# Experts after a recurrent layer: three of four token groups are normalised and turned behind the recurrent part's last tile, and the first expert's products are halved

## The reference, cut to what matters

```python
h = h + _L1_attn_ref(_layernorm(h), ...)      # the recurrence, all 32 x 192 rows
# step: Qh = h_prev - 2 v (v.h_prev)/(v.v);  h = lam*Qh + (1-lam)*x
h = h + _L1_ffn_ref(_layernorm(h), ...)       # the experts, rows 0..511 only
# gate_up = x[token] @ W_up[expert] + b; inter = (up+1) * gate*sigmoid(1.702*gate)
# down = inter @ W_down[expert] + b; out[token] += weight * down
```

## Time and profile before

| | |
|---|---|
| median of 3 runs | 1030.51 us (1027.21 to 1032.54) |
| the profiled execution | 1034.37 us, span in the trace 1032.6 us |
| PE busy, share of the span | 934.5 us, 91% |
| PE weight loads | 837.2 us, 81% |
| DVE | 786.5 us, 76% |
| ACT | 592.1 us, 57% |
| POOL | 545.4 us, 53% |
| granted clock of PE, mean | 0.957 of full speed |
| DMA | 96.32 MB, 93 GB/s over the span |

### The profile page before, as it was taken

One profiled execution on the slowest core, in us unless ns is written; L12 is line 12 of the kernel. 1 busy time (PEld: TensorE's weight loads), 2 busy tenths in 40 slices (PEclk: granted clock), 3 DMA queues, 4 the chain that ended last, 5 costly groups with the idle time before them and its releaser, 6 DMA issues. The chain is left out here.

```text
span 1032.6 us, 19334 instructions
## 1 busy us (share of the span) xinstructions
PE 934.5 (91%) x5800; PEld 837.2 (81%) x5800; DVE 786.5 (76%) x2393; ACT 592.1 (57%) x1174; POOL 545.4 (53%) x652
## 2 busy tenths in 40 slices
PE   2689999999999999869799999999999999963998
PEld 2689999999999999765587888887888888852887
DVE  3678777777777777652588898988999999972676
ACT  1346666666666666634566676666666666621442
POOL 4156676767676765445244454545555554422573
PEclk9889999999999999988989999999999999975999
DMA  5001111111111140012999999999999999982310
GB/s 208 21 26 42 42 42 41 41 41 41 41 41 41 44 171 22 17 27 76 102 128 142 149 159 139 157 141 152 151 156 150 146 163 141 135 96 94 123 62 21
DMA packets 134814, 96.32 MB, mean 93 GB/s; under 512 B 11208, under 2 KB 129104, under 8 KB 134096
## 3 DMA queue, kind: packets, MB, share of 16 engines
q1 hardware_dynamic: 133200, 91.20, 58.3%
q0 software_dynamic: 1536, 4.20, 1.4%
HBM read 31.92 MB, written 13.11 MB: 44 GB/s over the span
## 5 line engine op out<-in xcount | busy, mean ns | idle before, releaser
L315 POOL TENSOR_TENSOR gelu_lo<-gelu_out,gelu_hi 128x384 fp32r<-128x384 f32 x128 | 151.0, 1208 | 29.9 <-DVE gelu_hi L529 29.4
L944 POOL TENSOR_TENSOR B_decayed_u<-B_scan_in 128x512 f32<-128x512 f32 x48 | 62.0, 1292 | 97.1 <-DMA B_scan_in<-B_stage 88.5
L708 PE MATMUL psA<-ternary_down,gelu_hi 128*128 128x256 f32 x384 | 96.9, 291 | 6.9 <-POOL gelu_lo L315 6.3
L652 PE MATMUL psA<-x2T_hi,ternary_up 128*128 128x384 f32 x256 | 94.7, 370 | 3.4 <-DVE residual L642 3.2
L708 PE MATMUL psA<-ternary_down,gelu_lo 128*128 128x256 f32 x384 | 93.3, 282 | 0.0
L652 PE MATMUL psA<-x2T_lo,ternary_up 128*128 128x384 f32 x256 | 88.5, 346 | 0.0
L932 POOL TENSOR_TENSOR B_y<-B_scan_in,B_states 128x512 f32<-128x512 f32 x48 | 61.9, 1289 | 41.9 <-ACT B_states L1003 41.9
L1192 PEld LDWEIGHTS psB<-B_partial_dots,B_minus_same_batch 128*128 128x128 f32 x384 | 66.4, 194 | 21.8 <-DVE B_partial_dots L1076 10.6
L1180 PE MATMUL psB<-Win_hi,B_x_hi 128*128 128x512 f32 x192 | 83.6, 435 | 0.0
L708 PEld LDWEIGHTS psA<-ternary_down,gelu_hi 128*128 128x128 f32 x384 | 72.2, 188 | 11.4 <-POOL gelu_lo L315 10.2
L1092 DVE SCALAR_TENSOR_TENSOR psB<-B_decayed_u,psB 128x128 f32<-128x128 f32 x192 | 68.0, 354 | 12.7 <-PE psB L1192 12.2
(11 more groups left out here) (251 smaller groups left out, 3329.5 us busy)
## 6 DMA issues: line engine op xcount, KB each, us to landing
B_scan_in<-B_stage SPq DMA_DIRECT2D x192, 256.0 KB, 8.1
patches<-in_patches SPq DMA_DIRECT2D x16, 384.0 KB
B_residual<-layer_out SPq DMA_DIRECT2D x48, 128.0 KB, 5.2
out_dram<-B_residual SPq DMA_DIRECT2D x48, 128.0 KB, 5.0
C_raw<-in_experts SPq DMA_DIRECT2D x8, 768.0 KB, 4.4
layer_out<-residual SPq DMA_DIRECT2D x32, 128.0 KB, 1.8
layer_out<-residual SPq DMA_DIRECT2D x32, 64.0 KB, 2.0
raw_Wl<-in_upT SPq DMA_DIRECT2D x1, 1024.0 KB, 9.1
```

The source lines that it names most:

```text
L315: nc.gpsimd.tensor_tensor(act_l[:, k, :], act[:, k % DEEP, :], act_h[:, k, :].bitcast(F32), ALU.subtract).then_inc(s["ffn_lo"], 1)
L652: last = nc.tensor.matmul(out, a, b, start=(n == 0), stop=(n == len(terms) - 1))
L708: last = nc.tensor.matmul(ps[:, 6 + k // 2, (k % 2) * D:(k % 2 + 1) * D], x[:, c, k * P:(k + 1) * P], dn_w[:, c, :], start=(c == 0 and x i ...
L944: nc.gpsimd.tensor_tensor(lu[:, j % 2], ring[:, j % R_RING, :, LAM, :], ring[:, j % R_RING, :, U, :], ALU.mult).then_inc(s["lu"], 1)
```

## The change

Rows 0..511 are regrouped. Group q = 0, 1, 2 is now steps 0..127 of sequence q, and group 3 is steps 128..191 of sequences 0 and 1. The first three groups are complete once tile 31 is stored, long before part B ends. They become tiles 48, 49 and 50 of part B's normalisation: `has_x` lets the statistics, `rstd`, the normalised rows, the transposes and the split run on for three more tiles, and `x_tiles` puts their halves into part C's operand, which takes the place of the l weights (`Wl_Win_hi`, `Wl_Win_lo`, last used for tile 47). Part C's residual lies in `raw_Wv`, its two raw slots in `raw_Win` and `raw_Wl`, which part B no longer needs by then.

SP issues in part B, at `i = 30`, the constants (14 DMAs where there were 4, since the new groups are pieces of the old ones) and the weights of experts 0 and 1; at `i` = 39, 40 and 41 the rows of the three groups; at `i = 49` the 60 first rows of each half of group 3; and right behind the last residual update two copies of four rows each. ACT makes expert 0's high half at `i = 36`, POOL its low half at `i = 38`. The wait for the last stores moves from part B's end into part C. The semaphores are cleared at part B's start, and the clearing block and its barrier go away.

In part C, expert 0's `gate_up` is made in two halves of 256 columns: the first for groups 0 and 1 at once, then the turn of the routing weights, then the turn of group 3, then the second half. ACT normalises group 3 where DVE did before. The last store is five DMAs, three of them before the last group is done.

```diff
-        l_h, l_l = sb("Wl_Win_hi", [P, DC, DI], F32R), sb("Wl_Win_lo", [P, DC, DI], F32R)
+        l_h, l_l = E.x_h, E.x_l
...
+        def has_x(j):
+            return 0 <= j < TT + 3
+
+        def row_tile(j):
+            return res[:, j % R_RES, :] if j < TT else E.acc[:, j - TT, :]
+
+        def x_tiles(j):
+            if j < TT:
+                return x_h[:, j % 2], x_l[:, j % 2]
+            q = j - TT
+            return E.x_h[:, :, q * P:(q + 1) * P], E.x_l[:, :, q * P:(q + 1) * P]
...
+                if i == TT - 18:
+                    for a, b in ((E.b_up, io["up_bias"]), (E.b_dn, io["down_bias"])):
+                        sp.dma_start(a[:], b).then_inc(E.s["const_in"], 16)
...
+                    for a, b in ((E.picked, io["picked"]), (E.weights, io["routing"])):
+                        for q, lo, hi, q_in, lo_in in ((0, 0, P, 0, 0), (2, 0, P, 3, 0), (1, 0, 64, 1, 64), (1, 64, P, 2, 0),
+                                                       (3, 0, 64, 1, 0), (3, 64, P, 2, 64)):
+                            sp.dma_start(a[lo:hi, q, :], b[lo_in:lo_in + hi - lo, q_in, :]).then_inc(E.s["const_in"], 16)
+                    sp.wait_ge(s["w_lo"], 3)
+                    sp.wait_ge(s["m_ps"], 4)
+                    for e in range(2):
+                        sp.dma_start(E.raw[e], io["experts"][e]).then_inc(E.s["raw_in%d" % e], 16)
+                if i + 9 in range(TT, TT + 3):
...
+                    q = i + 9 - TT
+                    for j in range(28, 32):
+                        wait_stored(sp, j)
+                    sp.dma_start(E.acc[:, q, :], io["out"][q, 0:P, :]).then_inc(res_in[(TT + q) % 8], 16)
+                if i == TT + 1:
...
+                    for j in range(TT - 5, TT - 1):
+                        wait_stored(sp, j)
+                    for b in range(2):
+                        sp.dma_start(E.acc[b * (P // 2):b * (P // 2) + 60, 3, :],
+                                     io["out"][b, P:T - 4, :]).then_inc(E.s["h_in"], 16)
...
+                    if j == TT - 1:
+                        for b in range(2):
+                            sp.dma_start(E.acc[b * (P // 2) + 60:(b + 1) * (P // 2), 3, :],
+                                         res[4 * b:4 * b + 4, j % R_RES, :]).then_inc(E.s["h_in"], 16)
...
+                if i == TT - 10:
+                    pool.wait_ge(E.s["w_hi"], 1)
+                    nc.gpsimd.tensor_tensor(E.w_l[:], E.raw[0], E.w_h[:].bitcast(F32), ALU.subtract).then_inc(E.s["w_lo"], 1)
...
+                if i == TT - 12:
+                    sc.wait_ge(E.s["raw_in0"], 16)
+                    nc.scalar.activation(E.w_h[:], E.raw[0], ACT.Copy).then_inc(E.s["w_hi"], 1)
+                if has_x(i + 4):
...
-                    wait(pe, s["x_lo"], min(i + 5, TT))
+                    wait(pe, s["x_lo"], min(i + 5, TT + 3))
...
-        with nc.Block() as clearing:
-            @clearing.sync
-            def _(sp):
-                for sem_ in s.values():
-                    sp.sem_clear(sem_)
...
+            gate_up(0, slice(0, MT // 2))
+            pe.wait_ge(s["wc"], 1)
+            for q in range(MQ):
+                last = nc.tensor.transpose(ps[0:E_N, 6, q * P:(q + 1) * P], wc[:, q, :], ident[:])
+            last.then_inc(s["wcT"], 1)
+            pe.wait_ge(s["normed"], 1)
+            for c in range(DC):
+                last = nc.tensor.transpose(ps[:, c, 0:P], xn[:, c * P:(c + 1) * P], ident[:])
+            last.then_inc(s["xT"], 1)
+            pe.wait_ge(s["x_lo"], 1)
             for e in range(E_N):
-                gate_up(e)
+                gate_up(e, slice(MT // 2, MT) if e == 0 else slice(0, MT))
```

More of the change, by code:

```diff
@@ L854, in part_b @@
         arrived = [ctx.enter_context(nc.semaphore("B_arrived%d" % q)) for q in range(4)]
[L855 removed]
+        stored = E.stored = [E.stack.enter_context(nc.semaphore("B_stored%d" % q)) for q in range(4)]
+        for name in E.names:
+            E.s[name] = E.stack.enter_context(nc.semaphore("C_" + name))
         def wait_res_in(eng, j):
@@ L1028, in _ @@
                                          ACT.Copy).then_inc(s["y_hi"], 1)
-                if has(i + 4):
+                if has_x(i + 4):
                     j = i + 4
-                    wait(sc, s["z"], j - 1)
+                    wait(sc, s["z"], min(j - 1, TT))
                     sc.wait_ge(s["xT"], j + 1)
-                    nc.scalar.activation(x_h[:, j % 2], XT, ACT.Copy).then_inc(s["x_hi"], 1)
+                    nc.scalar.activation(x_tiles(j)[0], XT, ACT.Copy).then_inc(s["x_hi"], 1)
                 if i == -4:
@@ L1263, in part_c @@
         ident, halfpow = consts.ident, consts.halfpow
[L1264 to L1269, removed]
+        acc, raw, x_h, x_l = E.acc, E.raw, E.x_h, E.x_l
+        picked, weights, b_up, b_dn = E.picked, E.weights, E.b_up, E.b_dn
+        xn = sb("C_normed", [P, D])
+        stats, moments = sb("C_stats", [P, 6]), sb("C_moments", [P, 2])
+        ve, nmean = sb("C_var_eps", [P, 1]), sb("C_minus_mean", [P, 1])
+        rstd, shift = sb("C_rstd", [P, 1]), sb("C_shift", [P, 1])
+        picked_f = sb("C_picked_f", [P, MQ, 2])
         eq = sb("C_is_picked", [P, 2, MQ, E_N])
@@ L1297, in _ @@
         def _(sp):
-            sp.dma_start(acc[:], rows).then_inc(s["h_in"], 16)
-            for a, b in ((picked, io["picked"]), (weights, io["routing"]), (b_up, io["up_bias"]), (b_dn, io["down_bias"])):
-                sp.dma_start(a[:], b).then_inc(s["const_in"], 16)
-            for e in range(E_N):
-                if e >= 2:
-                    sp.wait_ge(s["w_lo"], e - 1)
-                sp.dma_start(raw[:, e % 2, :], io["experts"][e]).then_inc(raw_in[e % 2], 16)
+            for e in range(2, E_N):
+                sp.wait_ge(s["w_lo"], e - 1)
+                sp.dma_start(raw[e % 2], io["experts"][e]).then_inc(raw_in[e % 2], 16)
+            for q in range(4):
+                sp.wait_ge(E.stored[q], 16 * (T // 16))
+            for q in range(3):
+                sp.wait_ge(s["acc"], MQ * (E_N - 1) + q + 1)
+                sp.dma_start(io["out"][q, 0:P, :], acc[:, q, :]).then_inc(s["stored"], 16)
             sp.wait_ge(s["acc"], MQ * E_N)
-            sp.dma_start(rows, acc[:]).then_inc(s["stored"], 16)
-            sp.wait_ge(s["stored"], 16)
+            for b in range(2):
+                sp.dma_start(io["out"][b, P:T, :],
+                             acc[b * (P // 2):(b + 1) * (P // 2), 3, :]).then_inc(s["stored"], 16)
+            sp.wait_ge(s["stored"], 80)
         @block.gpsimd
@@ L1513, in program @@
         part_a(nc, W, io, consts)
-        part_b(nc, W, io, consts)
-        part_c(nc, io, consts)
+        E = Names()
+        E.stack, E.s = ctx, {}
+        E.names = """h_in const_in raw_in0 raw_in1 stats aggr ve rstd shift normed xT x_hi x_lo cast eq eq_sum wc wc_scaled wcT
+                wcT_copy bias bias_added w_hi w_lo gu b_up_one gate_b up_b silu act a_hi a_lo down acc stored""".split()
+        E.res = sb("B_residual", [P, 12, D])
+        E.x_h, E.x_l = sb("Wl_Win_hi", [P, DC, DI], F32R), sb("Wl_Win_lo", [P, DC, DI], F32R)
+        E.w_h, E.w_l = sb("C_w_hi0", [P, 6 * D], F32R), sb("C_w_lo0", [P, 6 * D], F32R)
+        E.picked, E.weights = sb("C_picked", [P, 4, 2], I32), sb("C_routing", [P, 4, E_N])
+        E.b_up, E.b_dn = sb("C_up_bias", [P, E_N, 4]), sb("C_down_bias", [E_N, D])
+        E.acc = W.raw_v[:].rearrange("p a b -> p (a b)")[:, 0:4 * D].rearrange("p (q d) -> p q d", d=D)
+        E.raw = [w[:].rearrange("p a b -> p (a b)")[:, 0:6 * D] for w in (W.raw_in, W.raw_l)]
+        part_b(nc, W, E, io, consts)
+        part_c(nc, E, io, consts)
 def kernel(x, x_txt, L0_tok_W, L0_tok_b, L0_txt_weight, L0_attn_wq, L0_attn_wk, L0_attn_wv, L0_ffn_w_up,
```

104 lines of the change are left out of this document (43 added, 61 removed).

## The result

The changed kernel takes 1014.91 us (median of 4 runs, 1013.88 to 1016.90), the kernel before 1029.40 us beside it: a ratio of 0.9859, 95% interval 0.9827 to 0.9891, or 14.5 us less. The forecast was 1026.2 us with a range of 1020 to 1033: wrong, too high by 11 us. The profiled execution took 1013.88 us, its span is 1012.1 us, 20.5 us less than the span before; 6.0 us of that is the choice of executions, since the profiled one of before lies 5.0 us over its median and this one 1.0 under.

What follows compares the result with a forecast made beforehand. Part B was taken as bound by PE's 8.55 us a tile and by full DMA engines, part C's start by a chain of waits. A gain of 13.7 us less 9.4 us of costs gave 4.3 us less: 1026.2 us, range 1020 to 1033.

Steps and rivals of the forecast that it cites:

- what part B costs: Sum of the change's costs in part B, 9.4 us, with next to no room in the DMA engines.
- the signs: What the trace after would show: part B's last update near 946 us; wrong if within 3 us of 936.9 or past 954.
- Rival 1: Part B: the DMA engines have room, so the loads cost 0 to 2 us; time 1021.5 us, chance 0.22.
- the gain in part C: From the last residual update to expert 1's start: 15.3 us in place of 28.45, a gain of 13.2 us.
- The first half: Part C, expert 0's first 24 products of 256 columns: 5.2 us at 1.2 GHz.
- Group 3: Part C: group 3 is ready by 8.5 us after the last update and hides behind expert 0's first half.
- The last store: End of part C: the last store in smaller pieces gains 0.5 us (0 to 1).
- the DMAs at i = 30: Part B: experts 4.0 us and constants 2.5 us ahead of tile 32's ring transfer; PE loses 6.0 us.
- rivals 2 and 4: At i = 30: experts at 145 GB/s, 14.4 us in all (chance 0.12); constants' small rows cost 8.2 us (chance 0.06).
- ACT's and POOL's splits: Part B: ACT's half of expert 0 costs 1.2 us ahead of the normalisation, POOL's half 1.5 us ahead of y.
- The drained end: Tiles 48 to 50 at part B's end: PE's output product waits for the low halves, 1.2 us (0 to 2).
- The -0.5 for ring waits saved later: Part B: ACT's and POOL's stalls let the DMA engines catch up, which saves 0.5 us of later ring waits.

Runs made afterwards that it cites:

- e1: The kernel before with one unused 32-byte piece ahead of the stage, so stage and ring start at a multiple of 256 bytes: ratio 0.988.
- e4: The kernel before with 32 unused bytes behind the stage, so the ring alone starts at a multiple of 256 bytes: ratio 0.987.
- e13: A repetition of e1 (the kernel before with stage and ring on multiples of 256 bytes): 1020.98 us, ratio 0.9857.
- e2: The changed kernel with 224 unused bytes ahead of the stage, so stage and ring start as in the kernel before: 1034.91 us, ratio 1.0015.
- e16: The kernel of e8 with 224 unused bytes ahead of the stage, so stage and ring start as in the kernel before: 1023.08 us, ratio 0.9858.
- e7: The changed kernel with only the 14 DMAs of the constants moved from iteration 30 to 45, behind the last ring transfer: 1010.09 us, ratio 0.9794.
- e8: The changed kernel with the experts' loads, the constants and expert 0's splits cut up over iterations of part B: 1005.76 us, ratio 0.9756.
- e5: The changed kernel with the loads of experts 0 and 1 and constants and expert 0's split moved to part C's start: 1026.99 us, ratio 0.9932.
- e11: The kernel before with the stage at a multiple of 256 bytes and the ring still 224 bytes behind one: ratio 1.0033.

## Why the prediction was wrong

- **Failed: what part B costs rests on the room in the DMA engines, and that was taken from the kernel before.** The prediction said that "the DMA engines, with a share of 1.24 at 145 GB/s in 785 to 793, are full", and "Whatever is added to them in part B has next to no room". It went through the diff by instructions and never by addresses. The buffers that moved ahead of part B put the ring on a multiple of 256 bytes. This term, which the sum puts at nothing without a reason, is 12 to 15 us in the runs (ratios of 0.988, 0.987 and 0.9857 in e1, e4 and e13, at 1030 us), and the miss is 11.3 us, 1.1 of which is that the kernel before stood at 1029.40 beside it and not at 1030.51. No rival contained it, and the last update stood at 931.2 us, below anything that the signs provided for. Rival 1 gave a time below the forecast for a wrong reason: there was no spare room in the kernel before, and with the old address ACT still waits for the ring in e2 and e16. Its premise that the share of 1.24 is that of the fullest engines is a misreading; it is the mean of the sixteen.
- **Right: the gain in part C**, 13.2 us forecast, 14.2 measured. The first half took 4.60 us (forecast 5.2 all at 1.2 GHz; the granted clock was 0.50 only from 935 to 938, 0.85 before and 0.91 behind that; the second half, at full clock, took 3.13). Group 3 was ready just in time: PE's turn of it waited 0.2 us for ACT. The last store cost nothing visible of the 0.5.
- **Right in size to a third, wrong in cause: the DMAs at i = 30.** 6.0 forecast, 8.2 measured. The prediction costed the constants at 2.5 us of the DMA engines and put SP's issues "inside the same 6.5". It is the reverse: e7 and e8 show 6.6 of the 8.2 us to be 14 issues, during which the DMA engines fall to 76 GB/s; the experts' bytes, for which it had 4.0, cost 1.6. With the ring on a multiple of 256 rivals 2 and 4 fall with it. With the old address, for which they were written, the same place lost 10.3 us in e2's trace, and no run divides that.
- **ACT's and POOL's splits:** 1.2 and 1.5 forecast, 1.13 and 0.87 measured; in e5, without them, both tiles are back at 8.53 and 8.55 us.
- **The drained end:** 1.2 forecast, 9.29 and 9.08 us for tiles 44 and 45 where they were 8.43 and 7.89, with 0.3 in tile 43 and 0.2 given back in tile 46: some 2.2 us. PE waits for the low halves of the added tiles, 0.97 us in each of the two, as was said.
- **The -0.5 for ring waits saved later:** there were none left to save.
- The terms as measured at the new address make -14.8 + 8.2 + 1.1 + 0.9 + 2.2 = -2.4 us, forecast -4.3. That these are near is in part luck, since the forecast's terms were meant for the old address. There e2 finds 1.0015, 1.5 us more than before (2 less to 5 more), so the sum would have missed there as well: for part B it has 9.4 us, and e2's trace 18.2.

These two rows, of the timeline of PE in the kernel after, are the cost in the drained end:

```profile
905.59 0.55 PE L1303 MATMUL psB<-Wout_hi,B_y_hi 128*128 128x256 f32 x1 [0.97 <-DVE Wl_Win_lo L1192]
...
914.68 0.55 PE L1303 MATMUL psB<-Wout_hi,B_y_hi 128*128 128x256 f32 x1 [0.97 <-DVE Wl_Win_lo L1192]
```

## What to carry to other kernels

Where the DMA engines are full, read the diff for addresses too: any buffer that is added, taken away or moved shifts those behind it, and 32 unused bytes were worth as much here as the rewrite gained at the kernel's end. There, put what a DMA writes in rows of 512 bytes on a multiple of 256. Before believing that a change gave a gain, undo the placement it brought along; and count small DMAs by their issues on the queue that the critical transfers share (0.58 us each), not by their bytes, and spread them over iterations behind the transfer that is waited for.

## What the runs showed of the hardware

- The start of the written rows of 512 bytes modulo 256: landing of 256 KB 6.5 to 6.7 us at 0, 7.4 to 7.7 at 64, 7.9 to 8.6 at 32, 128 and 224. The time may vary less as well: five executions of e1 and the four of e4 lie within 6.3 us each, the six of e13 within 7.4, the 23 of the kernel before beside e1 and e4 between 1023 and 1041 us. With so few executions that is a hint.
- The start of the rows read made no difference that helps (e11, ratio 1.0033).
- Issues of small DMAs took SP 0.58 us each (14 in 8.1 us), and the ring's next transfer stood behind them.
- Loads of 6,144 bytes a row ran beside the ring's at 360 GB/s in 766 to 771 of e7, with PE busy all the time; the two tiles there lost 1.6 us.
